# A two-layer graph network on one core: key gathers of two window pairs, folds by transposes, and a last step that writes the result

## The chip, the core and the metric

One core of a Trainium2 chip runs the whole kernel. The metric is the device time of an execution in microseconds. The engines are TensorE (PE; its weight loads are PEld), VectorE (DVE), ScalarE (ACT), GpSimd (POOL) and SyncE (SP); all DMA transfers of the core go through its 16 DMA engines, and SP, ACT and POOL each have a queue of them.

## What is computed

There are N = 12500 nodes with 32 features and E = 200000 edges sorted by target. Layer 0 is a message network, layer 1 ten steps of propagation:

```python
h = relu(layernorm(x))
m = relu(concat(h[src], edge_attr) @ w1a + b1a) @ w1b + b1b
s = segment_sum(m, dst); agg = s / max(cnt, 1)
x = x + (relu(concat(h, agg) @ w2a + b2a) @ w2b + b2b)
h = relu(layernorm(x)); f = h
for _ in range(10):
    f = segment_sum((f * out_deg**-0.5)[src], dst) * in_deg**-0.5
    f = 0.9 * f + 0.1 * h
x = x + f
```

## The kernel before

Nodes lie as 98 tiles (J) of 128 nodes. The kernel is a row of blocks, with all engines joined between them: loads and layer norm, degrees (sorted_degrees), prepare_sorted, messages_and_counts, nodes_of_runs, propagate, needs_general, store_result.

**messages_and_counts** goes over 98 groups g, each 16 edges of each of 128 partitions. POOL gathers a group's source rows with 16 indirect DMAs (L146) into one of seven row buffers, seven groups ahead; PE turns them (L1335, f32 transposes, eight per group in pairs) and multiplies them with the message weights (L1353), ACT applies relu, DVE sums the runs of equal targets (L1186). In the same groups DVE and PE count the edges between nodes: each group has a window group of edge keys, DVE makes one-hots from the keys (L1221, L1225), PE multiplies them (L1318, L1324), ACT packs the counts in 4 bits (L1259), SP stores them. The keys of a pair of groups (64 windows) come by one indirect DMA on POOL (L1077, fetch_keys) into 64 partitions, from offsets that DVE copies to key_idx (L1200) out of window_row; that table of window starts is made in prepare_sorted by matmuls (L1013) and a copy (L1003). PE turns the keys (L1293, turn_keys). The loop is `Fori` over 7 turns of BATCH = 14 groups, 7 pairs each; POOL runs 6 turns and half of a seventh, behind 6 key fetches and the first gathers. An order of waits written out by hand ties POOL to the engines: a step of POOL waits for the turned rows, the key pointer, the row index, then gathers.

**propagate** does ten steps, t = 0 to 9, in a `Fori` over five turns of two steps, side 0 and side 1, which use the two halves of `parts`. The features, scaled and split in three bf16 parts, are the stationary operand, the edge counts as fp8 the moving one. The 98 target tiles are: two (HEAD), then five blocks of 16 tiles swept with the counts, then 16 tiles whose sums come from gathered feature rows instead. A block is swept in 49 units of two source tiles (L2103, 24 matmuls of 512 columns per unit in four 32-column strips), a step is 245 units. SP loads the packed counts in 35 chunks per step through a ring of two (L1751), DVE opens each unit (L1917, L1918) into a ring of seven, and counts on PE's use of them. At a block's end ACT copies the sums from PSUM to `drain` (L1814), PE folds them (L2030: four f32 matmuls with the 128x128 identity times UNIT = 64, which also takes the scale out), and DVE makes the new features of 16 tiles: eight operations (new_features, L1948 to L1957), of which the last six scale and split them for the next step. ACT stores them as `feature_rows` (L1805). PE sweeps the first two units of the next block ahead of a fold. The gathered part: POOL gathers 256 times 128 feature rows per step (L1798), once the table of this step is wholly stored, into eight slots of four; PE uses them in 16 visits (L2077) between units, and folds their four banks with `stack`, identities of 32 columns times UNIT (L2054).

After step 9 PE sweeps two units and DVE opens nine of an eleventh step, SP loads two chunks for it, and ACT stores feature rows. SP has x brought back into the room of the gathered one-hots (L1769) and waits for all stores. needs_general computes a flag from counters on DVE and PE; store_result adds x to all 98 tiles (L879) and stores the result in two DMAs (L884, L885) of 128-byte rows.

## Time and profile before

| what | value |
|---|---|
| median of 3 runs | 6043.35 us (6040.39 to 6046.41) |
| the profiled execution | 6041.42 us |
| its span on the core | 6039.8 us, 196769 instructions |
| PE, DVE, POOL, ACT busy | 82%, 67%, 71%, 13% of the span |
| mean granted clock of PE | 0.905 of 2.4 GHz |
| HBM traffic | 775 MB read, 205 MB written |

The page cuts the span in 40 slices; a digit is the busy share in tenths:

```profile
PE   1675555555555553999999999999999999999997
DVE  7897766777776777666566666656666666665655
POOL 5777777777777764775767767676776767767675
PEclk9987777777777776999999999999999999999998
```

Slice 2 to 14 is messages_and_counts, from slice 16 on propagate. The share of the whole span mixes these two, so each is to be read by itself; a wait on an engine that does not set a stage's pace costs nothing.

### The profile page before, as it was taken

What the parts mean: (1) busy time and instruction counts of PE and PEld (TensorE: products, weight loads), DVE (VectorE), ACT (ScalarE), POOL (GpSimd) and SP (SyncE); (2) the same over time, 40 slices, a digit from 0 to 9 for tenths busy, and PEclk for the clock granted to TensorE, in tenths of its full rate; (3) what the DMA queues carried; (4) which work ended last, traced back from release to release, by engine and by line L of the source; (5) the groups of instructions that cost most, each with busy time, mean ns of one, the idle gap of its engine ahead of it and who ended that gap; (6) DMA issues with size and microseconds to landing.
All of it is one profiled execution on the core that took longest, in us unless ns stands there. A gap on an engine that the chain in (4) does not pass through costs nothing. (4 is left out here: it accounts for less than half of the span.)

```text
span 6039.8 us, 196769 instructions
## 1 busy us (share of the span) xinstructions
PE 4938.6 (82%) x76542; PEld 3090.9 (51%) x76542; DVE 4018.9 (67%) x11958; ACT 789.6 (13%) x1725; POOL 4296.1 (71%) x4300
## 2 busy tenths in 40 slices
PE   1675555555555553999999999999999999999997
PEld 1565455555555542555555555555555555555554
DVE  7897766777776777666566666656666666665655
ACT  0343333333333310000000000000000000000000
POOL 5777777777777764775767767676776767767675
PEclk9987777777777776999999999999999999999998
DMA  4543333333333312656556555555555556555655
GB/s 126 130 122 99 97 95 101 95 96 95 101 97 99 92 56 88 211 198 217 194 208 214 198 207 200 209 202 209 205 202 212 201 207 211 198 209 198 219 198 178
DMA packets 530050, 980.42 MB, mean 162 GB/s; under 512 B 295962, under 2 KB 461306, under 8 KB 483146
## 3 DMA queue, kind: packets, MB, share of 16 engines
q1 hardware_dynamic: 377002, 841.91, 39.8%
q0 software_dynamic: 136864, 97.04, 7.8%
q10 hardware_dynamic: 15232, 28.37, 1.3%
q8 instruction: 648, 10.62, 0.7%
q14 instruction: 304, 2.49, 0.1%
HBM read 775.11 MB, written 204.68 MB: 162 GB/s over the span
## 5 line engine op out<-in xcount | busy, mean ns | idle before, releaser
L1798 POOL DMA_INDIRECT x_nodes_fast<-feature_rows,x_nodes_fast x2560 | 2591.6, 1012 | 1050.6 <-issue 853.3
L2103 PE MATMUL banks_fast<-count_units_fast,feature_parts_fast 128*32 128x512 fp8e3 x58848 | 3230.6, 380 | 50.1 <-DVE gathered_hots L1983 34.4
L2103 PEld LDWEIGHTS banks_fast<-count_units_fast,feature_parts_fast 128*32 128x32 bf16 x58848 | 1586.8, 97 | 1592.7 <-issue 64.8
L1917 DVE TENSOR_SCALAR count_units_fast<-packed_ring_fast 128x512 int32<-128x512 int32 x2459 | 1063.8, 433 | 1332.7 <-PE banks_fast L2103 1291.2
L146 POOL DMA_INDIRECT rows_fast<-row_table,idx_fast x1456 | 1418.6, 974 | 443.7 <-issue 405.6
L1918 DVE TENSOR_SCALAR count_units_fast<-packed_ring_fast 128x512 int32<-128x512 int32 x2459 | 1055.8, 429 | 0.0
L1225 DVE TENSOR_SCALAR window_place_hot_fast<-iota_wide_fast,local_keys_fast,target_weight_fast 128x196 bf16<-128x196 f16 x3136 | 951.0, 349 | 0.0
L1335 PE MATMUL banks_fast<-identity_fast,rows_fast 128*128 128x128 f32 x784 | 221.2, 375 | 671.8 <-DMA rows_fast<-row_table,idx_fast 671.8
L1318 PE MATMUL banks_fast<-window_place_hot_fast,window_src_hot_fast 128*128 128x196 bf16 x3136 | 611.5, 282 | 21.9 <-DVE window_place_hot_fast L1225 14.8
L1324 PE MATMUL banks_fast<-window_place_hot_fast,window_src_hot_fast 128*128 128x196 bf16 x3136 | 596.3, 277 | 0.0
L1335 PEld LDWEIGHTS banks_fast<-identity_fast,rows_fast 128*128 128x128 f32 x784 | 97.8, 174 | 724.5 <-DMA rows_fast<-row_table,idx_fast 592.1
L1186 DVE SCALAR_TENSOR_TENSOR run_sums_fast<-run_sums_fast,same_target 128x96 f32<-128x96 f32 x1485 | 458.6, 309 | 7.6 <-issue 6.1
L1259 ACT CAST count_stage_fast<-banks_fast 128x392 uint16<-128x392 f32 x784 | 396.0, 505 | 294.0 <-PE banks_fast L1318 287.4
L1318 PEld LDWEIGHTS banks_fast<-window_place_hot_fast,window_src_hot_fast 128*128 128x128 bf16 x3136 | 400.8, 151 | 57.2 <-DVE window_place_hot_fast L1225 18.9
L1324 PEld LDWEIGHTS banks_fast<-window_place_hot_fast,window_src_hot_fast 128*128 128x128 bf16 x3136 | 402.0, 150 | 0.0
L1353 PE MATMUL banks_fast<-w1a_b1a_fast,turn_fast 49*128 49x96 f32 x3136 | 333.8, 342 | 61.1 <-ACT turn_fast L1264 60.3
L1353 PEld LDWEIGHTS banks_fast<-w1a_b1a_fast,turn_fast 49*128 49x128 f32 x3136 | 260.2, 232 | 141.8 <-issue 110.7
L1814 ACT COPY drained_fast<-banks_fast 128x512 f32<-128x512 f32 x50 | 29.4, 587 | 2214.9 <-PE banks_fast L2103 2214.9
L1220 DVE COPY idx_fast<-src_ends_fast 128x16 int32 x98 | 23.3, 238 | 426.7 <-PE banks_fast L1324 426.7
L1221 DVE TENSOR_TENSOR window_src_hot_fast<-iota_by_windows_fast,window_keys_fast 128x1024 bf16<-128x1024 bf16 x392 | 268.5, 685 | 10.4 <-PE banks_fast L1324 3.0
L1264 ACT COPY turn_fast<-banks_fast 128x256 f32<-128x256 f32 x392 | 145.7, 372 | 699.8 <-PE banks_fast L1335 689.6
L1268 ACT ACTIVATE run_sums_fast<-banks_fast 128x384 f32<-128x384 f32 x392 | 193.8, 494 | 264.6 <-PE banks_fast L1353 257.6
(315 smaller groups left out, 2187.4 us busy)
## 6 DMA issues: line engine op xcount, KB each, us to landing
packed_ring_fast<-edge_counts SPq DMA_DIRECT2D x352, 1792.0 KB
edge_counts<-count_stage_fast SPq DMA_DIRECT2D x100, 784.0 KB, 3.9
running_sums<-run_sums_fast SPq DMA_DIRECT2D x100, 768.0 KB, 3.6
x_nodes_fast<-feature_rows,x_nodes_fast POOLq DMA_INDIRECT x2560
rows_fast<-row_table,idx_fast POOLq DMA_INDIRECT x1456
feature_rows<-feature_parts_fast ACTq DMA_DIRECT2D x50, 384.0 KB
rows_fast<-attrs_padded SPq DMA_DIRECT2D x98, 128.0 KB
attrs_padded<-in_edge_attr SPq DMA_DIRECT2D x1, 12500.0 KB, 42.3
```

The source lines that it names most:

```text
L146: pool.indirect_dma_start(out=self.rows[:, r, c, 0:DN], out_offset=None, in_=b.dram.table, in_offset=bass.IndirectOffsetOnAxis(ap=idx[:, c ...
L1186: nc.vector.scalar_tensor_tensor(out=sums[:, s, c, :], in0=before, scalar=same[:, at], in1=sums[:, s, c, :], op0=ALU.mult, op1=ALU.add).th ...
L1225: nc.vector.tensor_scalar(place_hot[:, q % 2, w, :], iota_w[:, :], local[:, at:at + 1], weight[:, at:at + 1], ALU.is_equal, ALU.mult).then ...
L1259: nc.scalar.copy(to, of).then_inc(count_read, 1)
L1318: last = nc.tensor.matmul(b.banks[:, C_BANK[u % 4], side * WC:(side + 1) * WC], part_hot[:, m, :, w], place_hot[:, m, w, :], start=(half = ...
L1324: last = nc.tensor.matmul(b.banks[:, S_BANK, half * WC:(half + 1) * WC], part_hot[:, m, :, w], place_hot[:, m, w, :], start=False, stop=Fa ...
L1335: last = nc.tensor.transpose(b.banks[:, T_BANK, k * P:(k + 1) * P], rows[:, r_rows, c:c + 2, :].rearrange("p c d -> p (c d)"), b.ident[:, :])
L1353: last = nc.tensor.matmul(b.banks[:, M_BANK + k % 2, k // 2 * DH:(k // 2 + 1) * DH], turn[at:at + DI + 1, q % 2, (k // 2) * P:(k // 2 + 1) ...
L1798: pool.indirect_dma_start(out=rows[:, g % GSLOTS, i, :], out_offset=None, in_=b.dram.feature_rows[side], in_offset=bass.IndirectOffsetOnAx ...
L1917: nc.vector.tensor_scalar(to[..., 0:P // 8], of, NIBBLES, None, ALU.bitwise_and)
L1918: return nc.vector.tensor_scalar(to[..., P // 8:P // 4], of, 4, NIBBLES, ALU.logical_shift_right, ALU.bitwise_and)
L2103: last = nc.tensor.matmul(b.banks[at:at + DN, SWEEP[half_of(side, m)], 0:COLS], parts[:, side, j, k * DN:(k + 1) * DN], of_strip.bitcast(FP8),
```

## The change

Three edits. First, one key fetch brings the keys of two pairs, the second into partitions 64 to 127: four fetches for seven pairs (KEY_FETCHES = 4, the last for one pair), issued behind pairs 1, 3, 5 and 6 of a turn. window_row has 128 partitions, filled by two copies from twice as many matmuls; PE turns the keys of a pair with the left or right half of the identity. Second, a block's four folds are transposes with the plain identity; UNIT goes into `gain`, the factor of a target, and `stack` has plain ones. Third, the loops of SP, ACT, DVE and PE in propagate run four turns, and the last two steps follow written out; in the last one nothing is opened, swept or loaded for a later step, x comes back into the free half of `parts` at the step's third chunk, DVE makes the result of a block or bank with three operations (result), and ACT stores it at once, in 128-byte rows. needs_general's SP waits for these stores; store_result is no longer called here. The core of the diff (first prepare_sorted, then messages_and_counts, then propagate by engine, then the end):

```diff
+KEY_FETCHES = (AHEAD_GROUPS + 1) // 2
...
-            step(nc.vector.tensor_copy(window_row[:, 0:J // SLOTS], b.banks[0:SLOTS * WG, 2, 0:J // SLOTS]))
+            for half in range(2):
+                on = slice(half * SLOTS * WG, (half + 1) * SLOTS * WG)
+                by_loop = lambda t: t.rearrange("p (i f) -> p i f", f=KEY_FETCHES)[on, :, 0:KEY_FETCHES - half]
+                step(nc.vector.tensor_copy(by_loop(window_row[:, 0:J // BATCH * KEY_FETCHES]), by_loop(b.banks[:, 2, 0:J // BATCH * KEY_FETCHES])))
...
-            for k in range(SLOTS):
-                last = nc.tensor.matmul(b.banks[0:SLOTS * WG, 2, 0:J // SLOTS], first_of[:, k, :],
...
+            for half in range(2):
...
+                for k in range(SLOTS):
+                    last = nc.tensor.matmul(of_half, first_of[:, k, :],
+                                            start[:, :].rearrange("p (i a s) -> p s i a", a=AHEAD_GROUPS, s=SLOTS)[:, k, :, half::2],
...
-        key_idx = sb("key_idx", [LW, AHEAD_GROUPS], I32)
-        raw_keys = sb("raw_keys", [P, AHEAD_GROUPS, P, 2])
+        key_idx = sb("key_idx", [2 * LW, KEY_FETCHES], I32)
+        raw_keys = sb("raw_keys", [2 * LW, KEY_FETCHES, P, 2])
...
+        fetch_behind = {pair: pair // 2 for pair in (*range(1, AHEAD_GROUPS, 2), AHEAD_GROUPS - 1)}
...
-                pool.indirect_dma_start(out=raw_keys[0:LW, r, :, :].rearrange("p e k -> p (e k)"), out_offset=None,
+                pool.indirect_dma_start(out=raw_keys[:, r, :, :].rearrange("p e k -> p (e k)"), out_offset=None,
...
-                if t % SLOTS:
-                    pool.wait_ge(keys_pointed, k + 1)
+                if t % SLOTS and t // SLOTS in fetch_behind:
+                    r_keys = fetch_behind[t // SLOTS]
+                    pool.wait_ge(keys_pointed, i * KEY_FETCHES + (r_keys + 2))
                     pool.sem_inc(taken, 1)
-                    fetch_keys((t // SLOTS + KEYS_AHEAD) % AHEAD_GROUPS)
+                    fetch_keys(r_keys)
...
-            for r in range(KEYS_AHEAD):
+            for r in range(KEY_FETCHES):
                 fetch_keys(r)
...
-                        nc.vector.tensor_copy(key_idx[:, r_keys:r_keys + 1], window_row[:, bass.ds(k + AHEAD_GROUPS, 1)]).then_inc(keys_pointed, 1)
+                        if t // SLOTS in fetch_behind:
+                            r_keys = fetch_behind[t // SLOTS]
+                            nc.vector.tensor_copy(key_idx[:, r_keys:r_keys + 1],
+                                                  window_row[:, bass.ds((i + 1) * KEY_FETCHES + r_keys, 1)]).then_inc(keys_pointed, 1)
...
-            def turn_keys(r):
+            def turn_keys(pair):
+                r, half = divmod(pair, 2)
...
-                                            b.ident[:, 0:LW], start=True, stop=True, skip_group_check=True)
+                                            b.ident[:, half * LW:(half + 1) * LW], start=True, stop=True, skip_group_check=True)
...
-            with sp.Fori(0, steps2) as tt:
+            def load_two_steps(tt):
...
+                    if finishes(tt, side) and c == RING:
+                        sp.wait_ge(unit_used, UNITS + (STEPS - 1) * STEP_UNITS)
+                        sp.wait_ge(head_swept, STEPS - 1)
+                        sp.wait_ge(table_stored[0], 16 + (PAIRS - 1) * STORES * 16)
+                        sp.dma_start(x_again, b.dram.x_saved).then_inc(x_returned, 16)
...
-            for c in range(RING):
-                sp.wait_ge(opened, STEPS * STEP_UNITS + (c + 1) * UNITS)
-                load(c, c, 0)
-            sp.wait_ge(group_used, GSLOTS + (STEPS - 1) * STEP_GROUPS + (J * DN * 4 // P) // GROUP + 1)
-            sp.dma_start(x_back(hots), b.dram.x_saved).then_inc(x_returned, 16)
-            for slot in range(RING):
-                sp.wait_ge(chunk_in[slot], (STEPS * STEP_CHUNKS // RING + 1) * 16)
-            sp.wait_ge(x_returned, 16)
-            sp.wait_ge(table_stored[0], 16 + STEPS // 2 * STORES * 16)
-            sp.wait_ge(table_stored[1], STEPS // 2 * STORES * 16)
+            with sp.Fori(0, PAIRS - 1) as tt:
+                load_two_steps(tt)
+            load_two_steps(PAIRS - 1)
...
+            def store_result(where):
+                whole = min(where.stop, J - 1)
+                act.dma_start(out[P * where.start:P * whole, :].rearrange("(j p) d -> p j d", p=P),
+                              per_node(b.f[:, :])[:, where.start:whole, :]).then_inc(result_stored, 16)
+                if whole < where.stop:
+                    act.dma_start(out[P * whole:N, :], b.f[0:NL, whole * DN:(whole + 1) * DN]).then_inc(result_stored, 16)
+            def keep(t, side, where):
+                if finishes(t // 2 if isinstance(t, int) else t, side):
+                    store_result(where)
+                else:
+                    keep_rows(1 - side, where)
...
-            nc.vector.tensor_scalar(gain[:, :], b.dst_norm[:, :], 1.0 - ALPHA, None, ALU.mult).then_inc(prepared, 1)
-            nc.vector.tensor_scalar(eye[:, :], b.ident[:, :], UNIT, None, ALU.mult).then_inc(prepared, 1)
+            nc.vector.tensor_scalar(gain[:, :], b.dst_norm[:, :], 1.0 - ALPHA, UNIT, ALU.mult, ALU.mult).then_inc(prepared, 1)
...
+            def result(q, got, taken, done, where):
...
+                nc.vector.tensor_tensor(t1, per_node(got), gain[:, where].unsqueeze(2).broadcast_to([P, tiles, DN]), ALU.mult).then_inc(result_made, 1)
...
+                nc.vector.scalar_tensor_tensor(out=f, in0=h, scalar=ALPHA, in1=t1, op0=ALU.mult, op1=ALU.add).then_inc(result_made, 1)
...
+                dve.wait_ge(x_returned, 16)
+                nc.vector.tensor_tensor(f, f, x, ALU.add).then_inc(result_made, 1)
...
-                    last = nc.tensor.matmul(b.banks[:, FOLD[half], a * P:(a + 1) * P], drain[:, half, a * P:(a + 1) * P], eye[:, :],
-                                            start=True, stop=True)
+                    last = nc.tensor.transpose(b.banks[:, FOLD[half], a * P:(a + 1) * P], drain[:, half, a * P:(a + 1) * P], b.ident[:, :])
...
-                            sweep_units(t + 1, 0, 1 - side, 0, AHEAD)
+                            if not finishes(tt, side):
+                                sweep_units(t + 1, 0, 1 - side, 0, AHEAD)
                             fold_bank(t, GBANKS - 1)
...
+        @block.sync
+        def _(sp):
+            sp.wait_ge(result_stored, RESULT_STORES * 16)
...
-        propagate(nc, b, ins, parts, hots, unsorted)
-        needs_general(nc, b, counted_edges, crowded, unsorted, flag)
-        store_result(nc, b, out, x_back(hots))
+        propagate(nc, b, ins, out, parts, unsorted, result_stored)
+        needs_general(nc, b, counted_edges, crowded, unsorted, flag, result_stored)
```

## Rows read from the trace of the kernel before

**Rows 1.** Busy time by stretch: columns start:end, length, engines' busy (instructions), PEclk, DMA share, GB/s.
```profile
182.00:2160.00 1978.00, 1223.11 (x10389) 1054.57 (x10389) 1464.20 (x5637) 715.85 (x1573) 1495.40 (x1537) 0.76 0.37 101
...
5651.00:6005.00 354.00, 352.44 (x6479) 187.10 (x6470) 217.06 (x561) 5.63 (x10) 256.85 (x256) 1.00 0.59 208
```

**Rows 2.** Waits, 300 to 2100 us: engine line waited for: us, times, longest.
```profile
PE banks_fast L1335 <- DMA rows_fast<-row_table,idx_fast: 647.3, 81, 9.2
```

**Rows 3.** Timeline of POOL: start us, us, engine line op, tiles, count [idle before <-releaser].
```profile
2144.59 0.94 POOL L146 DMA_INDIRECT rows_fast<-row_table,idx_fast  x1 [0.30 <-issue]
```

**Rows 4.** Groups of instructions by line and form: xcount | busy, mean ns | idle before.
```profile
L146 POOL DMA_INDIRECT rows_fast<-row_table,idx_fast x1456 | 1418.6, 974 | 443.7 <-issue 405.6 <-ACT count_stage_fast L1259 35.7 <-DVE idx_fast L1220 1.8
...
L1077 POOL DMA_INDIRECT raw_keys_fast<-edge_keys,key_idx_fast x51 | 47.4, 930 | 15.5 <-issue 15.5
...
L2030 PE MATMUL banks_fast<-unit_identity_fast,drained_fast 128*128 128x128 f32 x400 | 57.7, 288 | 0.0
```

**Rows 5.** Timeline, end of the preparation, DVE and POOL.
```profile
153.71 0.20 DVE L1003 CAST window_row<-banks_fast 64x49 int32<-64x49 f32 x1
...
154.63 0.94 POOL L146 DMA_INDIRECT rows_fast<-row_table,src_ends_fast  x1 [0.30 <-issue]
```

**Rows 6.** Timeline of PE: a fold in the propagation, a pair of transposes in messages.
```profile
3056.02 1.16 PE L2030 MATMUL banks_fast<-unit_identity_fast,drained_fast 128*128 128x128 f32 x8
...
3057.01 0.53 PE L2041 MATMUL banks_fast<-stacked_identities_fast,head_drained_sums_fast 128*128 128x32 f32 x4
...
1208.60 0.44 PE L1335 MATMUL banks_fast<-identity_fast,rows_fast 128*128 128x128 f32 x2
...
1208.88 0.33 PE L1318 MATMUL banks_fast<-window_place_hot_fast,window_src_hot_fast 128*128 128x196 bf16 x2
```

**Rows 7.** Waits, 2480 to 6006 us, the propagation.
```profile
POOL x_nodes_fast L1798 <- DMA feature_rows<-feature_parts_fast: 137.0, 5, 34.7
...
DVE count_units_fast L1917 <- DMA packed_ring_fast<-edge_counts: 21.7, 10, 2.7
...
PE banks_fast L2077 <- DMA x_nodes_fast<-feature_rows,x_nodes_fast: 11.2, 10, 2.0
...
PE banks_fast L2103 <- issue: 5.6, 4, 1.7
```

**Rows 8.** Timeline of the end, and the last wait of SP's queue.
```profile
6001.05 0.59 ACT L1814 COPY drained_fast<-banks_fast 128x512 f32<-128x512 f32 x1 [0.84 <-PE banks_fast L2103]
...
6003.44 0.97 PEld L2054 LDWEIGHTS banks_fast<-stacked_identities_fast,x_nodes_fast 96*128 96x128 f32 x8 [0.42 <-issue]
...
6004.56 0.29 DVE L1948 TENSOR_TENSOR scaled_fast<-banks_fast,target_gain_fast 128x128 f32<-128x128 f32 x1 [0.23 <-PE banks_fast L2054]
...
6007.27 0.69 DVE L1948 TENSOR_TENSOR scaled_fast<-banks_fast,target_gain_fast 128x512 f32<-128x512 f32 x1 [0.23 <-DVE feature_parts_fast L1955]
...
6011.94 0.43 DVE L1955 CAST feature_parts_fast<-scaled_fast 128x512 bf16<-128x512 f32 x1
...
6015.45 0.15 DVE L2176 TENSOR_SCALAR bad_rows<-most_edges 128x1 f32<-128x1 f32 x1 [3.08 <-PEq L1678]
...
6017.77 0.14 DVE L2188 CAST general_flag<-bad_rows 1x1 int32<-1x1 f32 x1
...
6018.44 3.43 DVE L879 TENSOR_TENSOR f_nodes_fast<-f_nodes_fast,gathered_hots 128x3136 f32<-128x3136 f32 x1 [0.53 <-PEq L2172]
...
6022.34 10.80 SPq L885 DMA_DIRECT2D out_nodes<-f_nodes_fast  x1
...
SPq L876 <- DMA out_nodes<-f_nodes_fast: 1.3, 1, 1.3
```

**Rows 9.** DMA issues by line: count, KB each, median us to landing.
```profile
gathered_hots<-x_saved SPq DMA_DIRECT2D x1, 1568.0 KB, 11.2
```

**Rows 10.** Timeline of PE in messages: transposes after a wait, and later.
```profile
1200.37 0.69 PE L1335 MATMUL banks_fast<-identity_fast,rows_fast 128*128 128x128 f32 x2 [8.45 <-DMA rows_fast<-row_table,idx_fast]
...
1206.24 0.44 PE L1335 MATMUL banks_fast<-identity_fast,rows_fast 128*128 128x128 f32 x2
```

More of the change, by code:

```diff
@@ L1032, in messages_and_counts @@
         attrs_in = [sem(f"attrs_in{r}") for r in range(AHEAD_GROUPS)]
-        keys_in = [sem(f"keys_in{r}") for r in range(AHEAD_GROUPS)]
+        keys_in = [sem(f"keys_in{r}") for r in range(KEY_FETCHES)]
         sums_out = [sem(f"sums_out{s}") for s in range(SLOTS)]
@@ L1720, in propagate @@
         BANK_COLS = BANK_TILES * P
-        steps2 = STEPS // 2
+        PAIRS = STEPS // 2
+        finishes = lambda tt, side: isinstance(tt, int) and 2 * tt + side == STEPS - 1
         CHAIN = 2 + 2 * SPLITS
@@ L1783, in _ @@
                 pool.wait_ge(stacked, k + 1)
-                nc.gpsimd.affine_select(out=stack[:, :], in_=stack[:, :], compare_op=ALU.not_equal, fill=UNIT,
+                nc.gpsimd.affine_select(out=stack[:, :], in_=stack[:, :], compare_op=ALU.not_equal, fill=1.0,
                                         base=-k * DN, pattern=[[-1, DN]], channel_multiplier=1).then_inc(stacked, 1)
             pool.wait_ge(idx_made, 1)
-            with pool.Fori(0, steps2) as tt:
+            with pool.Fori(0, PAIRS) as tt:
                 for side in range(2):
@@ L1853, in _, with two_steps @@
             act.sem_inc(bank_drained, 2)
-            with act.Fori(0, steps2) as tt:
+            def two_steps(tt):
                 for side in range(2):
@@ L1876, in _ @@
                     keep_block(t, side, 4)
+            with act.Fori(0, PAIRS - 1) as tt:
+                two_steps(tt)
+            two_steps(PAIRS - 1)
         @block.vector
@@ L1933, in open_unit @@
                              packed[:, (side * STEP_CHUNKS + c) % RING, :, u * UJ:(u + 1) * UJ, :].bitcast(I32)).then_inc(opened, 1)
+            def result(q, got, taken, done, where):
+                tiles = where.stop - where.start
+                t1 = per_node(scaled[:, 0:tiles * DN])
+                f, h, x = (per_node(of)[:, where, :] for of in (b.f[:, :], b.h[:, :], x_again))
+                nc.vector.tensor_tensor(t1, per_node(got), gain[:, where].unsqueeze(2).broadcast_to([P, tiles, DN]), ALU.mult).then_inc(result_made, 1)
+                dve.wait_ge(result_made, q * 3 + 1)
+                dve.sem_inc(taken, 1)
+                nc.vector.scalar_tensor_tensor(out=f, in0=h, scalar=ALPHA, in1=t1, op0=ALU.mult, op1=ALU.add).then_inc(result_made, 1)
+                dve.wait_ge(result_made, q * 3 + 2)
+                dve.wait_ge(x_returned, 16)
+                nc.vector.tensor_tensor(f, f, x, ALU.add).then_inc(result_made, 1)
+                dve.wait_ge(result_made, q * 3 + 3)
+                dve.sem_inc(done, 1)
             def new_features(q, side, got, taken, done, where):
+                if isinstance(q, int) and q >= (STEPS - 1) * FEATS:
+                    return result(q - (STEPS - 1) * FEATS, got, taken, done, where)
                 tiles = where.stop - where.start
@@ L1997, in _, with two_steps @@
             dve.wait_ge(hots_made, GATHERS // PIECE)
-            with dve.Fori(0, steps2) as tt:
+            def two_steps(tt):
                 for side in range(2):
@@ L2007, in _ @@
                                 open_unit(tt, 1, v - STEP_UNITS)
-                            else:
+                            elif not finishes(tt, side):
                                 open_unit(tt + 1, 0, v - STEP_UNITS)
@@ L2020, in _ @@
                             q = q + 1
+            with dve.Fori(0, PAIRS - 1) as tt:
+                two_steps(tt)
+            two_steps(PAIRS - 1)
         @block.tensor
@@ L2162, in _, with needs_general @@
                             fold_head(t)
-            for strip in range(STRIPS):
-                nc.tensor.matmul(b.banks[strip * DN:(strip + 1) * DN, SWEEP[0], 0:COLS], b.zeros16[:, 0:DN],
-                                 b.zeros16[:, :].unsqueeze(1).broadcast_to([P, COLS // P, P]), start=False, stop=True)
-def needs_general(nc, b, counted_edges, crowded, unsorted, flag):
+            with nc.Fori(0, PAIRS - 1, engines=[pe.engine], hint_back_edge=True) as tt:
+                two_steps(tt)
+            two_steps(PAIRS - 1)
+def needs_general(nc, b, counted_edges, crowded, unsorted, flag, result_stored):
     with nc.semaphore("flag_made") as made, nc.semaphore("flag_turned") as turned, \
```

44 lines of the change are left out of this document (23 added, 21 removed).

## The prediction

> **What bounds the kernel now.** I read the busy times by stretch first, because the kernel has two long stages with different limits. From 182 to 2160 us (messages and edge counts) PE is busy 1223 of 1978 us, DVE 1464, POOL 1495; in one step of the propagation (the last, 5651 to 6005) PE is busy 352.4 of 354 us at granted clock 1.00 and POOL 257 [rows 1]. Busy alone does not settle the first stage, so the waits come next: from 300 to 2100 us PE waited 647.3 us, in 81 groups, for gathered rows, and nothing else is of that size [rows 2]. The timeline of POOL says why: it issues one gather after another with only some 0.30 us of issue between them (443.7 / 1456) [rows 4], until the last one at 2144.59 [rows 3]. A row gather thus costs (1418.6 + 443.7) / 1456 = 1.279 us of POOL, a key gather (47.4 + 15.5) / 51 = 1.233 us [rows 4]. That stage is POOL's issue rate; a propagation step is PE's matmul rate; the end (from 6001 on) is a serial chain.
>
> **1. Key gathers by halves.** Before, POOL issues 6 + 6 x 7 + 3 = 51 of them [rows 4], each into 64 partitions. After: 4 ahead of the loop, 6 x 4 in it, and 1 in the last partial turn (only pair 1 of pairs 0 to 2 fetches) = 29, each into all 128. The price of a 128-partition key gather is not in the trace. Its nearest row is the row gather of the same POOL, 128 offsets, 1.279 us; the lower end is today's 1.233. The upper end is double the busy part of today's, 2 x 0.93 + 0.30 = 2.16, if POOL paid by bytes. I take 1.279, as a gather of 64 offsets is busy 0.93 us on average and one of 128 0.97 [rows 4]: offsets hardly count. Sum: 51 x 1.233 - 29 x 1.279 = 62.9 - 37.1 = 25.8 us; ends 27.1 (22 x 1.233) and 0 (29 x 2.16 = 62.6). As POOL is gapless up to 2144.59 [rows 3] and PE follows it by a landing, I count all of it. What is late next: still POOL, since a group costs it 16 x 1.279 = 20.5 us and PE waits 647.3 / 81 = 8 us in each. No wait is added: POOL's wait on the key pointers sits where one sat, and DVE sets the pointer in the same place, in 28 of 49 pairs (21 copies fewer, all in DVE's idle time). A fetch is issued about six pairs before its turn, some 240 us at 1978 / 98 = 20.2 us a group [rows 1]. The preparation gets a second DVE copy and four more PE instructions ahead of a block's end; today's copy starts at 153.71 while POOL's last gather there starts at 154.63 and runs to 155.57 [rows 5], so they hide; uncovered they would cost 0.3 us.
>
> **2. Folds by transposes.** 400 matmul records are 8 for each of 50 block folds, two per f32 matmul [rows 4]. The eight of a fold start at 3056.02 and hand PE over at 3057.01: 0.99 us. A transpose of the same tile is one record: the pair at 1208.60 hands over at 1208.88, 0.28 us, of which the first weight load is about 0.06 and each transpose 0.11 [rows 6]. Four are 0.06 + 4 x 0.11 = 0.50 us, so a fold loses 0.49 us, and 50 folds 24.5 us. The multiplication by UNIT moves into the gain made once; the three drains and the feature chains keep their lengths. The scaled identity's one DVE operation goes (0.3 us at most, in a stage where DVE waits for POOL and loads).
> Not all of 24.5 arrives. PE already waited ten times, 11.2 us in all, for gathered feature rows, and POOL cannot run ahead: five times it sat some 27 us each for the stored table at a step's start [rows 7]. Where PE arrives 0.5 us earlier at such a visit it waits 0.5 us longer: 10 x 0.5 = 5 us given back. I take 20; ends 5 (four of the five folds in every step given back: they lie between the table's store and the last visit) and 24.5.
> The clock stands at 1.00 through a whole step [rows 1] although PE waits up to 2.0 us there [rows 7]. The Trainium skill, "TensorE: Matmul & The Clock Gate", Part 4 (PE-mode transpose), speaks against this edit twice: it gives about 275 ns for a 128x128 transpose in context and says that transposes don't count as PE-busy for the clock. By its 275 ns a fold of four would take 1.1 us and gain nothing, an estimate from that page; rows 6 show such a length for a single record but hand-over after 0.11 us, so on the length the measurement decides. The rule on the clock is a rival, below.
>
> **3. The end of the last step.** Today: block 4's last sweep is drained from 6001.05 to 6001.64; two units of a step that is never used run until the bank fold begins at 6003.44; DVE starts the bank's features at 6004.56, the block's at 6007.27, and ends them at 6012.37; a store of feature rows nobody reads lands and the next block's DVE starts at 6015.45 and ends at 6017.91; then x is added (3.43 us) and the whole result stored from 6021.9, with the second store's issue until 6033.14 and SP's wait 1.3 us longer, 6034.4; 5.4 us follow to the end at 6039.8 [rows 8].
> After: the unused two units go, so the bank fold begins 2.45 us earlier (6000.99) and its features at 6002.1. They are three operations instead of eight: about 1.1 us, to 6003.2. The block fold waits for the drain (6001.64) and the bank fold and ends near 6002.5, so the block starts at 6003.3 and takes three of its operations, 2.3 us: 6005.6. The block ends with no landing to wait for: barrier 0.5 to 1 us, check chain 2.46 us, done near 6009. Beside it lands the last store, 256 KB in 128-byte pieces: the whole result, 1552 KB, took 12.1 us (6022.3 to 6034.4), so 2.0 us in proportion, and I put 2.2 us before it for issue and landing (ends 0 and 4; the last store of today, 384 KB, was in within 3.1): 5.7 + 4.2 = 6009.9. With the same 5.4 us after it, 6015.3. Saved: 39.8 - 15.3 = 24.5 us; ends 21 and 27.
>
> **4. What the written-out steps cost: 0.** x comes back in chunk 2 of the last step, ahead of that chunk on SP's queue. The load took 11.2 us when it shared the queue [rows 9]; behind it wait the chunk loads, behind those DVE's unpacking, behind that PE. DVE's unpacked units run seven ahead of PE (10 us, at 354 us for 245 units [rows 1]), and chunk loads are late only ten times, 21.7 us in all [rows 7], so over 5 us of a chunk's lateness is covered. Uncovered it would cost PE up to 4 us once. The result's stores of 2048 pieces replace stores of feature rows on ACT; ACT's next drain may wait about 2 us behind one, under a block of 70 us with two banks. One turn of PE's loop goes, of whose turns four show issue idle of 5.6 us together [rows 7]: a gain of 1.4 if the fall-through costs nothing, a loss as large if it does. I put 0, ends -2 and +5.
>
> **Sum.** 25.8 + 20 + 24.5 = 70.3 us. The profiled execution took 6041.42 us with a span of 6039.8, 1.6 outside it; after: span 5969.5, execution 5971.1. The median of the three runs lies 1.9 above the profiled execution, so the median after is 6043.35 - 70.3 = 5973.0.
>
> **Rivals.**
> A, the gathers bind the propagation. POOL needs 256 gathers in a step and begins them only once the table is stored; for it: PE waits on them already, ten times [rows 7]; against: the waits are short, and POOL idles 27 us per step. Then 5 of the 24.5 us are left: 5973 + 15 = 5988.
> B, a 128-partition key gather costs POOL double. For: twice the bytes per gather; against: 128 row offsets take hardly more than 64 keys. Part 1 gains 0: 5973 + 26 = 5999.
> C, transposes cost what they last, not what they hand over. Fold gain 0: 5973 + 20 = 5993. Against: rows 6.
> D, everything arrives: folds 24.5, a loop turn 1.4, end 27, keys 27.1: 80.0 saved, 5963.
> E, slower than before: the clock falls at the folds. After a wait of 8.45 us PE's transposes ran at half pace (0.69 us for the pair at 1200.37) and were at full pace (0.44) again at 1206.24, under 6 us later [rows 10]. If each fold let the clock fall, 3.5 us of sweep at half the rate would cost 1.75 us, 50 x 1.75 = 88, and the fold gain is in no sweep. 5973 + 88 = 6061, above before by 18; it decides from 70.3 / 1.75 = 40 of the 50 folds on. Against it stands the clock at 1.00 beside pauses as long as a fold. This is what the page's rule on the clock would do here (same part of the Trainium skill); no row can show it, as no transpose stands in a full sweep.
> F, the written-out steps stall (x ahead of the chunks, small stores among the gathers, code that comes late): 10 us, 5983.
>
> **How the numbers follow.** Forecast 0.53; A 0.17, D 0.12, F 0.07, B 0.05, C 0.04, E 0.02. The forecast's own range is 5966 to 5982. The range for 8 in 10 takes in A, most of D and F and leaves out B, C and E: 5960 to 5991. 0.2% (about what a measurement of this kernel can tell) is 12 us. All but E are faster by more: faster 0.97, same 0.01, slower 0.02.
>
> **What would show it.** In the profile after: 29 key gathers of about 0.95 us busy and the last row gather near 2119; PE's wait on rows still some 8 us a group; the first stage shorter by 25 us. The fold's records 200, not 400, a fold 0.50 us from start to hand-over; more waiting of PE for gathered feature rows than 11.2 us (A if above 25); clock 1.00 in the steps (E if not). The end: from the last drain of a block to the end of the span 14.3 us instead of 38.8. It is wrong if key gathers take over 1.5 us, if the step's length falls by under 1 us, or if the last two steps are longer than those before.

## The result, and the profile after

The changed kernel takes 5988.78 us (median of four runs, 5986.43 to 5989.91) against 6043.39 us for the kernel before: a ratio of 0.9909, 95% interval 0.9892 to 0.9926, so 55 us less. The forecast was 5973.0, with 5960 to 5991 as the range: the time lies inside it, 16 us above the forecast, and within 1 us of rival A (5988). The profiled execution took 5986.43 us with a span of 5984.8.

First the stage of the gathers: rows of the groups by line and form (count | busy, mean ns | idle before), and the last row gather on POOL's timeline. They answer to [rows 3, 4].

```profile
L147 POOL DMA_INDIRECT rows_fast<-row_table,idx_fast x1456 | 1411.0, 969 | 443.8 <-issue 414.8 <-ACT count_stage_fast L1270 28.4 <-DVE idx_fast L1231 0.3
L1085 POOL DMA_INDIRECT raw_keys_fast<-edge_keys,key_idx_fast x29 | 28.8, 993 | 8.8 <-issue 8.8
L2082 PE MATMUL banks_fast<-identity_fast,drained_fast 128*128 128x128 f32 x200 | 32.6, 285 | 0.0
```

```profile
2111.77 0.94 POOL L147 DMA_INDIRECT rows_fast<-row_table,idx_fast  x1 [0.30 <-issue]
```

There are 29 key gathers instead of 51, each (28.8 + 8.8) / 29 = 1.30 us of POOL, and the last row gather starts 32.8 us earlier (2144.59 before). The fold's records are 200 instead of 400.

The propagation is next. First gather to last gather, from the row that sums up one line (duration ns min/median/max, first and last start):

```profile
L1809 POOL DMA_INDIRECT x_nodes_fast<-feature_rows,x_nodes_fast x2560: 940/989/34317, 2343.0 to 5960.2; - x197
```

```profile
L1798 POOL DMA_INDIRECT x_nodes_fast<-feature_rows,x_nodes_fast x2560: 940/989/34225, 2374.2 to 5990.7; - x197
```

The first row is of the changed kernel, the second of the one before: 3617.2 us against 3616.5. The ten steps are not one microsecond shorter, although each fold is. PE's waits there (us, times, longest), to be held against the 11.2 and 5.6 of [rows 7] and against the last row here, which is of the kernel before (the head sweep is its line 2116):

```profile
PE banks_fast L2128 <- DMA x_nodes_fast<-feature_rows,x_nodes_fast: 23.4, 14, 3.7
PE banks_fast L2167 <- issue: 13.0, 9, 1.8
PE banks_fast L2154 <- issue: 5.7, 4, 1.9
...
PE banks_fast L2116 <- issue: 1.1, 2, 0.9
```

"Issue" idle is time in which PE stood still and waited for nothing that the profile shows.

The end, on the timeline from the last drain on, and SP's last wait ([rows 8] before):

```profile
5971.97 1.08 PE L2105 MATMUL banks_fast<-stacked_identities_fast,x_nodes_fast 96*128 96x32 f32 x8
5972.09 0.58 ACT L1840 COPY drained_fast<-banks_fast 128x512 f32<-128x512 f32 x1 [0.84 <-PE banks_fast L2154]
5972.79 0.49 PEld L2082 LDWEIGHTS banks_fast<-identity_fast,drained_fast 128*128 128x128 f32 x4
...
5974.29 0.69 DVE L1970 TENSOR_TENSOR scaled_fast<-banks_fast,target_gain_fast 128x512 f32<-128x512 f32 x1
...
5976.70 0.40 ACTq L1822 DMA_DIRECT2D out_nodes<-f_nodes_fast  x1
5977.57 0.15 DVE L2229 TENSOR_SCALAR bad_rows<-most_edges 128x1 f32<-128x1 f32 x1 [1.02 <-PEq L1686]
...
5979.89 0.14 DVE L2241 CAST general_flag<-bad_rows 1x1 int32<-1x1 f32 x1
```

```profile
SPq L2225 <- DMA out_nodes<-f_nodes_fast: 2.5, 1, 2.5
```

From the last gather to the end of the span it is 5984.8 - 5960.2 = 24.6 us; before, 6039.8 - 5990.7 = 49.1.

So of the 55.0 us of span, 31.2 come ahead of the propagation (first feature gather 2374.2 before, 2343.0 after), 24.5 from the end, and -0.7 from the ten steps. The question for the experiments was where the folds' 24.5 us went.

### The profile page after: what moved, and what is told of

Read it like the earlier page. It is cut to its first block and busy times, and to the rows that moved or that the text cites. A ratio compares the mean times of both kernels' runs of the same rounds, so it can differ in the third digit from the quotient of the medians.

```text
span 5984.8 us, 194809 instructions
## 1 busy us (share of the span) xinstructions
PE 4906.0 (82%) x76294; PEld 3060.0 (51%) x76294; DVE 3992.9 (67%) x11868; ACT 787.8 (13%) x1725; POOL 4272.7 (71%) x4278
## 3 DMA queue, kind: packets, MB, share of 16 engines
q8 instruction: 645, 10.57, 0.7%
## 5 line engine op out<-in xcount | busy, mean ns | idle before, releaser
L147 POOL DMA_INDIRECT rows_fast<-row_table,idx_fast x1456 | 1411.0, 969 | 443.8 <-issue 414.8
L1330 PE MATMUL banks_fast<-window_place_hot_fast,window_src_hot_fast 128*128 128x196 bf16 x3136 | 607.7, 280 | 22.0 <-DVE window_place_hot_fast L1236 14.6
L1231 DVE COPY idx_fast<-src_ends_fast 128x16 int32 x98 | 25.5, 260 | 403.7 <-PE banks_fast L1336 403.7
```

The costliest lines, as they stand in the source:

```text
L147: pool.indirect_dma_start(out=self.rows[:, r, c, 0:DN], out_offset=None, in_=b.dram.table, in_offset=bass.IndirectOffsetOnAxis(ap=idx[:, c ...
L1330: last = nc.tensor.matmul(b.banks[:, C_BANK[u % 4], side * WC:(side + 1) * WC], part_hot[:, m, :, w], place_hot[:, m, w, :], start=(half = ...
```

## The experiments

Runs 1 to 4, 5 to 8 and 9 to 12 shared a chip each; ratios are to the kernel before on the same chip (6050.13, 6051.66 and 6049.5 us). The changed kernel itself was timed beside a kernel before of 6043.39 us, so what sets a run apart from it is read from the ratios and not from the medians; each ratio is uncertain by about 0.0017, and the difference of two by some 0.0024, 15 us. Differences of single profiles are given as from the first to the last fold. Edits are to the changed kernel where nothing else is said. Diffs are shortened.

**Folds as matmuls again.**

```diff
-                    last = nc.tensor.transpose(b.banks[:, FOLD[half], a * P:(a + 1) * P], drain[...], b.ident[:, :])
+                    last = nc.tensor.matmul(b.banks[:, FOLD[half], a * P:(a + 1) * P], drain[...], b.ident[:, :], start=True, stop=True)
```

> The changed kernel with the 50 block folds as f32 matmuls with the plain identity again (400 records, 0.99 us a fold), all else as changed. Theory 1: in the changed kernel the 24.5 us of the folds came back as PE's waits, 12 us more for gathered rows (23.4 against 11.2 us) and 12 us of issue idle in the head sweep (13.0 against 1.1 us); then undoing the folds costs nothing: 5989 us, within 3, with issue idle at the head sweep near 1 and gather waits near 11. Theory 2: the folds do bring their 20 us and something else in the changed kernel lost them: 6009 us.

Measured: 5990.27 us, ratio 0.9901 (0.9885 to 0.9918), against 0.9909 with transposes. Taking the fold's gain away costs nothing that can be measured; from the first to the last fold the profile has 3530.7 us against 3527.9. PE's waits in this kernel:

```profile
PE banks_fast L2128 <- DMA x_nodes_fast<-feature_rows,x_nodes_fast: 13.1, 10, 2.1
PE banks_fast L2154 <- issue: 7.1, 5, 2.1
PE banks_fast L2167 <- issue: 2.2, 4, 0.8
```

Both takers shrink with it: rows of features 23.4 to 13.1, head sweep 13.0 to 2.2. Together that is 21 us of the 24.5, less 1.4 us by which the unit sweeps' issue idle grew (5.7 to 7.1).

**Transposes with two small instructions ahead of each**, so that the fold has as many instructions on PE's queue as before:

```diff
                 for a in range(TILES // STRIPS):
+                    pe.sem_inc(passed, 1)
+                    pe.sem_inc(passed, 1)
                     last = nc.tensor.transpose(...)
```

> The changed kernel with two semaphore increments of PE's queue before each transpose, eight a fold, so that PE's stream holds as many instructions as with the matmul folds and its 16 KB pieces begin where they did. Theory 1a: where the pieces of PE's instructions begin decides the 13 us of issue idle at the head sweep: it falls to about 1 to 5 us, and the time falls by 0 to 10 us, 5979 to 5989, less by what the gathers take back. Theory 1b: the idle there is DMA traffic at that moment, not place: idle stays near 13, time 5989 to 5995 (the increments themselves cost at most 50 x 8 x 0.02 = 8 us).

Measured: 5983.11 us, 0.9890 (0.9874 to 0.9907); head sweep idle 6.7 us, gathered rows 18.4, unit sweeps 10.2. Adding 400 instructions did no harm (11 us less by the ratios, inside their uncertainty; 8 us less from first to last fold), and the idle time in the head sweep halved, to somewhat more than the 1 to 5 us expected. The places of rest in the head sweep say why this is about the instructions themselves. Timeline of PE, the head sweep of 294 matmuls (start, us, count, idle before): one step of the kernel before, two of the changed one, one of this kernel.

```profile
2617.57 3.35 PE L2116 MATMUL banks_fast<-head_counts_fast,feature_parts_fast 128*32 128x256 fp8e3 x115
2621.12 5.09 PE L2116 MATMUL banks_fast<-head_counts_fast,feature_parts_fast 128*32 128x256 fp8e3 x179 [0.20 <-issue]
```

```profile
2584.76 3.56 PE L2167 MATMUL banks_fast<-head_counts_fast,feature_parts_fast 128*32 128x256 fp8e3 x123
2590.05 4.88 PE L2167 MATMUL banks_fast<-head_counts_fast,feature_parts_fast 128*32 128x256 fp8e3 x171 [1.73 <-issue]
2946.83 2.25 PE L2167 MATMUL banks_fast<-head_counts_fast,feature_parts_fast 128*32 128x256 fp8e3 x75
2950.87 6.18 PE L2167 MATMUL banks_fast<-head_counts_fast,feature_parts_fast 128*32 128x256 fp8e3 x219 [1.79 <-issue]
```

```profile
2590.31 3.24 PE L2169 MATMUL banks_fast<-head_counts_fast,feature_parts_fast 128*32 128x256 fp8e3 x111
2593.80 3.68 PE L2169 MATMUL banks_fast<-head_counts_fast,feature_parts_fast 128*32 128x256 fp8e3 x128 [0.25 <-issue]
2597.84 1.71 PE L2169 MATMUL banks_fast<-head_counts_fast,feature_parts_fast 128*32 128x256 fp8e3 x55 [0.36 <-issue]
```

The pause stands at the same matmul in every other step (at 123 in the changed kernel; 106 in the last of them, which is written out) and at 75 in those between (the last step has none), and where there are two they are 128 matmuls apart, which with their weight loads are 256 instructions. With the padding it stands at 111, where it also stands in the kernel with matmul folds. So the pause goes with a place in the instruction stream. The larger of two queues named "instruction" in the profile moves pieces of that size (the other, q14, moved 296 of 8.2 KB):

```profile
q8 instruction: 645, 10.57, 0.7%
```

10.57 MB in 645 packets is 16.4 KB each. The Trainium skill, "Advanced Engine Details and Errata", section Sequencer and Instruction Queues (ISA Cache), gives a line of 16 KB, 256 instructions; the rows agree with it, and by it PE stood at the borders of such lines. The page has no price for a border; in the head sweeps of the kernel before and the changed one it was 0.2 to 1.8 us. The times of the queue's packets bear the reading out: in the fourteen profiles PE's 145 pauses on issue in the ten steps all ended 2.2 to 3.0 us after the start of a packet of q8 (median 2.4), where these packets come 6.7 us apart on average. In the changed kernel one starts at 2587.67, and PE goes on at 2590.05. So the pauses are waits for PE's own instructions.

**Three of four gathers, with transposes.** One gather in each group of the propagation is left out and PE uses its neighbour's rows, so the edges of every fourth row set are not summed.

```diff
                         for i in range(GROUP):
+                            if i == GROUP - 1:
+                                continue
```

> The changed kernel with three of four feature row gathers issued in the propagation (192 a step, 4 x 16 fewer per 16 visits); PE multiplies the third row of a group twice, so its work is the same, and the fourth row's edges are left out. Waits for gathered rows must vanish. If the gathers are what took the fold gain back (rival A), the time falls by 12 to 23 us, to 5966 to 5977; if the instruction supply alone did, it falls by under 5.

Measured: 5966.53 us, 0.9865 (0.9849 to 0.9881). PE waits for no gathered row; what is left:

```profile
PE banks_fast L2169 <- issue: 14.1, 14, 1.7
PE banks_fast L2156 <- issue: 6.7, 4, 2.3
```

**The same with matmul folds.**

> As the run with three of four gathers, with the folds as f32 matmuls. Set against that run it is what a transposed fold is worth where no gather is late: 24.5 us more if PE's time alone counts, 12 more if the issue idle at the head sweep belongs to the transposed version, 0 if some third thing sets the step.

Measured: 5972.71 us, 0.9875 (0.9858 to 0.9891); head sweep 2.4 us, unit sweeps 7.3. Without the gathers in the way the fold is worth about 6 us by the medians (same chip, the two sets of times do not overlap), between the 12 and the 0 expected; it is 12.3 from first to last fold record in the profiles (3499.0 against 3511.3); another 11.1 are issue idle (20.8 against 9.7). That is 23.4 of 24.5.

**Head sweep in 14 pieces of 21 matmuls, behind units 2 to 15 of the next block**, so that PE uses up its instructions less fast there:

```diff
+        HEAD_PIECES = 14
...
                     sweep_units(t, m, side, v, v + 1)
+                    if m == HEAD_AFTER + 1 and AHEAD <= v < AHEAD + HEAD_PIECES:
+                        sweep_head(t, side, v - AHEAD)
...
-                        if m == HEAD_AFTER:
-                            sweep_head(t, side)
```

> The changed kernel with the head sweep (294 matmuls in one row behind block 2's fold) cut in 14 pieces of 21 matmuls, one behind each of units 2 to 15 of block 3: the same work, but PE never takes its instructions faster than some 40 a microsecond for long. If the 13.0 us of issue idle in the head sweep come from PE using instructions faster than they are brought, that idle goes to under 3 us. The time then falls by up to 13 us if nothing else binds, and by only 2 to 6 us (5983 to 5987) if the gathers take the rest back, with waits for gathered rows rising from 23 to 28 us or more.

Measured: 5982.76 us, 0.9886 (0.9869 to 0.9902).

```profile
PE banks_fast L2129 <- DMA x_nodes_fast<-feature_rows,x_nodes_fast: 24.4, 15, 3.8
PE banks_fast L2155 <- issue: 6.8, 5, 2.3
PE banks_fast L2169 <- issue: 0.5, 2, 0.3
```

The head sweep's idle time is gone (13.0 to 0.5) and the gathers keep theirs (24.4). Of the 12.5 us the ratios show 14, with an uncertainty as large, and the profile 6.5 from first to last fold (3527.9 to 3521.4). That the head sweep's idle went is shown; how much of it reached the time is not settled.

**Pieces and three of four gathers together.** (The same edges are left out as above.)

> The head sweep in 14 pieces and three of four gathers (PE multiplies the third row of a group twice; the fourth row's edges are left out). With both suspected takers gone: the run with three of four gathers (5966) less its 14.1 us of issue idle in the head sweep, 5953 +- 3. If the idle only moves to the unit sweeps, 5964 to 5967.

Measured: 5949.19 us, 0.9831 (0.9814 to 0.9847), with 0.8 us of idle in the head sweep and 7.0 in the unit sweeps. Both takers away, it is 0.34% (20 us, uncertain by 15) below the three of four gathers with transposes alone; from first to last fold it is 14.6 us (3499.0 to 3484.4), for 13.3 us that left the head sweep.

**All gathers, pieces, and PE's visits to gathered rows later** (the first nine by two units, the rest by one).

```diff
-        visit_unit = lambda visit: (303 + 146 * visit - (54 if visit >= 9 else 0)) // 10
+        visit_unit = lambda visit: (323 + 146 * visit - (64 if visit >= 9 else 0)) // 10
```

> The head sweep in pieces, and the 16 visits to gathered rows moved later: the first nine by two units (2.6 us), the rest by one. All gathers are there. If PE's waits for gathered rows come from visits placed before the rows are in, and not from POOL's rate over a whole step, they fall from above 23 us to under 8, and the time comes to 5960 to 5970. If POOL's rate over the step binds, the waits move to later visits and the time stays at 5983 to 5989.

Measured: 5964.75 us, 0.9858 (0.9842 to 0.9875). It computes all that the kernel before computes and beats both: 87 us below before and, by the ratios, 0.5% (31 us) below the change. PE's waits:

```profile
PE banks_fast L2155 <- issue: 13.9, 10, 3.5
PE banks_fast L2129 <- DMA x_nodes_fast<-feature_rows,x_nodes_fast: 3.3, 7, 1.2
```

**The kernel before with the key gathers alone.** The diff is that of part 1.

> The kernel before with the key gathers by halves alone. By the sum of rows: 51 x 1.233 - 29 x 1.29 = 25 us less, and 3 either way by the scatter of long row gathers (the last row gather came at 2111.8 to 2118.5 in five profiles with it, 2144.6 in the one without). Theory 2, that this edit gave all of 33 us by itself: ratio to before 0.9945. By the sum 0.9958.

Measured: 6020.40 us, 0.9950 (0.9933 to 0.9967): 30 us less, plus or minus 10. That lies between the sum of rows (0.9958) and the 33 us of theory 2 (0.9945), and excludes neither.

**The kernel before with the folds alone.** The diff is that of part 2.

> The kernel before with the folds by transposes alone (key gathers, loops and end as before; the scale in the gain). By the recorded forecast 20 us less: ratio 0.9967. By what the changed kernel showed (24.5 us of PE's time given back as waits for gathered rows and as issue idle in the head sweep) 0 to 4 us less: ratio 0.9993 to 1.0000, with issue idle in the head sweep above 8 us.

Measured: 6054.45 us (10 runs), 1.0007 (0.9998 to 1.0017). The folds by themselves are worth nothing that can be measured: between 1 us less and 10 us more, where the forecast had 20 less. PE's waits, and on its timeline one head sweep:

```profile
PE banks_fast L2075 <- DMA x_nodes_fast<-feature_rows,x_nodes_fast: 21.2, 12, 2.8
PE banks_fast L2114 <- issue: 13.7, 10, 1.7
PE banks_fast L2101 <- issue: 7.9, 4, 2.2
```

```profile
2626.78 3.67 PE L2114 MATMUL banks_fast<-head_counts_fast,feature_parts_fast 128*32 128x256 fp8e3 x127
2631.80 5.05 PE L2114 MATMUL banks_fast<-head_counts_fast,feature_parts_fast 128*32 128x256 fp8e3 x167 [1.35 <-issue]
```

The border moved from matmul 115 to 127: three folds stand ahead of the head sweep in the first step of a turn, each with 4 x 2 instructions less, 24 in all, or 12 matmuls with their loads. The count fits exactly. It fits in the second step of a turn too, where eight folds stand ahead, worth 32 matmuls: from 171 with padded folds to 203 in the changed kernel, and one line of 128 before that is the 75 seen.

**The seventh kernel with matmul folds.**

> The version with the head sweep in pieces and later visits, its folds as f32 matmuls. If the two takers are all that stood against the transposes, this is 24.5 us slower than that version with transposed folds (5965 on its chip): ratio to before 0.9858 + 0.0041 = 0.990. If the step is set by something else, the ratio stays at 0.986.

Measured: 5971.58 us, 0.9875 (0.9859 to 0.9892), where the transposes had 0.9858. The intervals overlap: the ratios give the fold 10 us with an uncertainty of 15, so that 24.5 is only just at the edge, and from first to last fold it is 5.2 us (3507.4 to 3502.2). Its waits show where the rest is:

```profile
PE banks_fast L2155 <- DVE count_units_fast L1949: 3.1, 3, 1.2
PE banks_fast L2155 <- issue: 2.1, 4, 0.9
```

No wait for gathered rows stands in the list, and issue idle is 2.1 us where the transposes have 13.9. My reading that a spread head sweep would cure the issue idle was too simple: with transposes it turned up in the unit sweeps. Most of what this version gains over the changed kernel comes with either kind of fold: with matmul folds the same placing takes 3530.7 us from first to last fold down to 3507.4.

**The end alone** (parts 1 and 2 undone; the folds are matmuls, with the scale still in the gain).

> The changed end alone: last two steps written out, no sweep and no table for an eleventh step, the result stored by blocks; key gathers and matmul folds as in the kernel before. The recorded sum gives 24.5 us less, ratio 0.9959; from the last block's drain to the end of the span some 14 us.

Measured: 6026.29 us, 0.9962 (0.9948 to 0.9976): 23 us less, as forecast.

**The later visits alone**, head sweep in one row.

> The changed kernel with the 16 visits later (nine by two units, the rest by one), the head sweep in one row. The waits for gathered rows (23.4 us) fall to about 5 us, the issue idle in the head sweep stays at about 13: 5989 less up to 18, so 5970 to 5975, ratio 0.987 to 0.988. If the placing works only together with the cut head sweep, 5985 or more.

Measured: 5982.14 us, 0.9891 (0.9875 to 0.9908): 11 us below the change by the ratios, inside their uncertainty, 14.6 from first to last fold; the expectation of 5970 to 5975 was missed.

```profile
PE banks_fast L2154 <- issue: 15.8, 8, 3.3
PE banks_fast L2167 <- issue: 8.7, 4, 2.7
PE banks_fast L2128 <- DMA x_nodes_fast<-feature_rows,x_nodes_fast: 1.5, 2, 1.3
```

The wait for rows is gone (23.4 to 1.5), the issue idle rose by 5.8 (18.7 to 24.5), and POOL's wait for PE rose from 33 to 58 us. Later visits alone do not explain that rise: in the version with both edits, where the visits stand in the same places, it is 36 us.

**One account for all.** From the first to the last fold record of each profile, less PE's waits listed between them, stands what PE did by itself. In us; the kernels with the old end have 2.45 us for its two unused units taken off as well.

| kernel | first to last fold | waits for rows | issue idle | other waits | rest |
|---|---|---|---|---|---|
| before | 3528.6 | 11.2 | 6.7 | 1.3 | 3506.9 |
| keys alone | 3530.0 | 11.0 | 9.0 | 0.8 | 3506.7 |
| end alone | 3521.8 | 7.9 | 9.2 | 1.5 | 3503.2 |
| matmul folds | 3530.7 | 13.1 | 9.3 | 0 | 3508.3 |
| spread, later, matmul folds | 3507.4 | 0 | 2.1 | 3.9 | 3501.4 |
| after | 3527.9 | 23.4 | 18.7 | 0.5 | 3485.3 |
| folds alone | 3532.3 | 21.2 | 21.6 | 0.8 | 3486.2 |
| padded folds | 3519.8 | 18.4 | 16.9 | 0 | 3484.5 |
| spread | 3521.4 | 24.4 | 7.3 | 0.4 | 3489.3 |
| later | 3513.3 | 1.5 | 24.5 | 0.8 | 3486.5 |
| spread, later | 3502.2 | 3.3 | 13.9 | 1.6 | 3483.4 |
| three of four gathers, matmul folds | 3511.3 | 0 | 9.7 | 0 | 3501.6 |
| three of four gathers | 3499.0 | 0 | 20.8 | 0 | 3478.2 |
| three of four gathers, spread | 3484.4 | 0 | 7.8 | 0.2 | 3476.4 |

With all gathers the five rests with matmuls have a mean of 3505.3, the six with transposes 3485.9: 19.4 us less, of the 24.5 that 50 folds lose. The four pairs that differ in the folds give 20.7, 23.0, 18.0 and, with three of four gathers, 23.4. Where the other 1 to 6 us are was not found. It is the two columns of waits that decide how much reaches the time.

## Why the prediction was right or wrong

**Part 1, the key gathers: right.** Said 25.8. The rows give 62.9 - 37.6 = 25.3, the price being 1.30 us where I took 1.279. Done alone, the time says 30 plus or minus 10. The last row gather starts at 2144.6, 2149.3 and 2153.1 in the three profiles of kernels without the edit (before, end alone, folds alone) and at 2111.8 to 2119.8, mean 2116.3, in the eleven with it: 32.7 us. The 7 us more than the rows of the key gathers are in the row gathers, busy 1418.6 to 1427.6 us without it and 1411.0 to 1419.3 with it. Why they are some 5 ns shorter each was not tested. PE still waits for them 632.0 us in 82 groups, as said. Rival B is refuted: a key gather into 128 partitions is busy 0.99 us, not 1.86.

**Part 2, the folds: their length right, the amount given back wrong.** The fold itself went from 0.99 to 0.49 us between start and hand-over:

```profile
3025.24 0.66 PE L2082 MATMUL banks_fast<-identity_fast,drained_fast 128*128 128x128 f32 x4
3025.73 0.53 PE L2092 MATMUL banks_fast<-stacked_identities_fast,head_drained_sums_fast 128*128 128x32 f32 x4
```

So rival C is refuted. The step that failed is "10 x 0.5 = 5 us given back": the waits rose by 12.2 us (11.2 to 23.4), with single ones up to 3.7. It counted 0.5 us for each of the ten waits that I saw, as if the waits stayed where they were. They did not. Before, all ten stand at the fourth and fifth of a step's 16 visits. In the changed kernel 14.2 of the 23.4 us are five waits at the second visit, one in every other step, where the kernel before has none. That visit before (first row) and after:

```profile
2824.69 1.09 PE L2077 MATMUL banks_fast<-gathered_hots,x_nodes_fast 128*96 128x128 fp8e3 x16
...
2792.39 0.87 PE L2128 MATMUL banks_fast<-gathered_hots_fast,x_nodes_fast 128*96 128x128 fp8e3 x12
2795.84 0.40 PE L2128 MATMUL banks_fast<-gathered_hots_fast,x_nodes_fast 128*96 128x128 fp8e3 x4 [2.58 <-DMA x_nodes_fast<-feature_rows,x_nodes_fast]
```

Counted from the start of the last fold of the step before, PE comes there 0.5 us earlier (57.7 instead of 58.2 us), and the visit's last gather starts 0.8 us later (54.8 instead of 54.0), as the first gather of the step is busy 4.5 instead of 3.8 us. All six profiles with transposes and all gathers have this last gather at 54.8 us or later in those steps, and a wait at this visit; the five with matmul folds have it at 54.0, and no wait there. Why that first gather is longer, and why 1.3 us of lost margin became 2.6 us of wait, is open. No block fold stands between the start of the step's gathers and this visit, so the waits are not what several folds had saved since then: my lower end ("four of the five folds in every step") is not borne out as a reason either. In kind it is rival A, PE waiting for gathers that can begin only once the table is stored. That the waits take a part of the gain is shown by the three-of-four-gathers runs and by the later visits: without the late rows the wait is gone and the time between the folds falls.

The other 12 us went to a taker that neither sum nor rivals had: issue idle of PE, 6.7 to 18.7 us, nearly all of it in the head sweep (1.1 to 13.0). I read the 5.6 us of issue idle in [rows 7] as the turn of the loop and did not ask what else could sit in PE's own supply of instructions. The alone-run of the folds shows that both takers come from the folds and from nothing else in the change: 21.2 and 21.6 us. That A's number fitted to 1 us is thus half luck: A has 19.5 us given back to the gathers, and 12 were. The prediction's own sign of being wrong, a step's length that falls by under 1 us, has come about: the ten steps together are 0.7 us longer. Rival D, that everything arrives, is out by the same.

What stays open: why a border costs 0.2 us in one kernel and 1.7 in another. The place counts (the padded folds have the old places, and 6.7 us instead of 13.0 in the head sweep) but does not settle it, as matmul folds with the same places have 2.2. How fast PE used up the instructions before it seems to count (a head sweep goes through 128 matmuls in 3.7 us). But when spread, the pauses came back in the unit sweeps as 13.9 us, one of 3.5 us. Which place is good was not found, nor what sets the start of the fetch.

**Part 3, the end: right.** Said 24.5; 24.5 in the profile, 23 in the run alone. The pieces: the chain of checks 2.46 us from 5977.57 to 5980.03, the barrier 1.02, the block's DVE 2.2 us behind the drain's start (said 2.3). From the last drain on it is 12.7 us instead of the 14.3 that I said, as the span ends 8.1 us after the last store's issue (5976.70) where I had 9.6 (4.2 + 5.4); but the drain comes 11.9 us after the last gather instead of 10.4. The two cancel. Small errors on both sides, and a right sum partly by that.

**Part 4, the written-out steps: right at 0.** The x load waits for PE's sweep for 8.9 us on SP's queue; DVE's waits for chunks are 25.5 us in ten instead of 21.7 [rows 7], and PE shows no wait for it. The issue idle in the unit sweeps stays at 5.7 us in four. Rival F is out.

**Rival E** is refuted: the granted clock is 1.00, the level of 2.4 GHz, from 2600 to 5950 us with 46 of the 50 groups of transposes in it. Two readings in that rival were loose: rows 10 have the pair at 0.69 against 0.44 us, 1.6 times and not twice (the granted clock was 0.50 and 1.00 there), and the 3.5 us of sweep in its price stand in none of the rows.

```profile
2600.00:5950.00 3350.00, 3308.26 (x60786) 1772.06 (x60778) 2054.33 (x5276) 51.80 (x92) 2383.00 (x2381) 1.00 0.59 206
```

**Sum.** Terms as said and as found in the profiled span: first stage 25.8, found 31.2; folds 20, found -0.7; end 24.5, found 24.5. The excess of the first made up a part of what the second lacked: with 25.3 there the time would have been near 5995, above the range. The three parts alone multiply to 0.9950 x 1.0007 x 0.9962 = 0.9919, against 0.9909 (0.9892 to 0.9926) for all: they add up.

## What to carry to other kernels

Time that an engine saves in front of a wait for a stream can be given back, and by more than the waits that are seen let one count: here 12.2 us instead of 5, most of it at a visit that had no wait before. Ask at which visits rows come just in time, not only where the engine already waits. Where an engine runs at 99% with short instructions, its own supply of them can be a second limit: look at the places of "issue" idle, and if they repeat at the same count of instructions, a change in the number of instructions moves them, for better or worse. The shorter fold was worth nothing measurable alone (1.0007). With the head sweep in pieces and later visits the kernel comes to 0.9858 instead of 0.9909, but that placing gives most of it with matmul folds too (0.9875), so it is the first thing to try.

## What the runs showed of the hardware

- PE stood idle on issue at fixed places 128 short matmuls (256 instructions) apart, for 0.2 to 2.7 us in the head sweep (2.7 in the kernel with later visits alone) and up to 3.5 us in a unit sweep; 24 instructions fewer moved the place by 12 matmuls. All of it together was 2.1 to 24.5 us in ten steps, between kernels whose sweeps do the same work. All 145 such pauses in the fourteen profiles ended 2.2 to 3.0 us after the start of a 16.4 KB packet of the queue "instruction".
- Four f32 transposes of 128 by 128 hand PE over after 0.49 us at the granted clock 1.00 (2.4 GHz), four such matmuls after 0.99. The Trainium skill, "TensorE: Matmul & The Clock Gate", Part 4 (PE-mode transpose), gives about 275 ns for one, stated beside a bf16 figure; the records do last 273 ns (median), but they overlap, and the hand-over sets the cost.
- An indirect gather of 128 offsets is busy 0.97 to 1.00 us on average, whether it fetches rows or, into twice as many partitions as before, keys (64 partitions: 0.93); POOL's share of one hardly depends on the offsets here. The first gather behind a freshly stored table took longer: 3.8 us in every other step of the kernel before, 4.5 in the changed one.
